# A 16-stage hybrid network on one core: order of the weight loads, loading of x, two attention openings, and a connection network in three bf16 parts

## What is computed

```
L0a mamba block + small MLP    L0f ternary layer     L0b attention, 16 narrow heads   L0g ternary layer
L1a linear attention           L1f connection net    L1b attention, 64-wide heads     L1g connection net
L2a one-head attention         L2f top-2 experts     L2b causal narrow attention      L2g top-2 experts
L3a mamba block                L3f gated (SiLU) net  L3b ReLU attention by sorting    L3g gated net
```

```python
def _conn_dense(kernel_bool, x):
    w = jnp.where(kernel_bool, jnp.float32(1.0), jnp.float32(-1.0))
    return x @ w
h = jnp.concatenate([x, -x], axis=-1)
h = s0 * _conn_dense(k0, h)          # 256 -> 512
h = jax.nn.relu(h) * 2
h = s1 * _conn_dense(k1, h)          # 512 -> 512
h = jax.nn.relu(h) * 2
h = s2 * _conn_dense(k2, h)          # 512 -> 128
```

## Time and profile before

| | us |
|---|---|
| runs: median (lowest, highest) of 3 | 3164.71 (3163.57, 3168.61) |
| the profiled execution's own time | 3165.05 |
| its span, first to last instruction | 3163.5 |
| mean granted clock of TensorE | 0.927 |

### The profile page before, as it was taken

One profiled execution on the slowest core, in us unless ns is written; L12 is line 12 of the kernel. 1 busy time (PEld: TensorE's weight loads), 2 busy tenths in 40 slices (PEclk: granted clock), 3 DMA queues, 4 the chain that ended last, 5 costly groups with the idle time before them and its releaser, 6 DMA issues. The chain is left out here.

```text
span 3163.5 us, 33520 instructions
## 1 busy us (share of the span) xinstructions
PE 2570.9 (81%) x11730; PEld 1095.1 (35%) x11738; DVE 1586.3 (50%) x2507; ACT 1446.3 (46%) x2392; POOL 677.6 (21%) x644
## 2 busy tenths in 40 slices
PE   3777788999789789768767787889997897897677
PEld 1231244544344234223222213445443442342232
DVE  3967543555121631695649585245442117217955
ACT  3544614555334354554545355155552444445454
POOL 1732010000001521371227311000000024115520
PEclk9898989999979899899889989999998898998998
DMA  3002000000010210000000010000000102100000
GB/s 122 1 1 73 8 1 1 1 1 1 1 53 1 76 59 0 0 1 1 1 15 1 25 56 1 1 1 1 1 1 0 53 1 81 54 0 1 0 1 7
DMA packets 36751, 55.68 MB, mean 18 GB/s; under 512 B 7648, under 2 KB 19936, under 8 KB 36576
## 3 DMA queue, kind: packets, MB, share of 16 engines
q1 hardware_dynamic: 32224, 49.53, 4.8%
q10 hardware_dynamic: 4352, 3.94, 0.4%
HBM read 39.54 MB, written 13.63 MB: 17 GB/s over the span
## 5 line engine op out<-in xcount | busy, mean ns | idle before, releaser
L522 POOL TENSOR_TENSOR xs<-xs,L2f_part 128x512 f32<-128x512 f32 x32 | 40.5, 1264 | 1181.8 <-DVE L2f_part L511 1181.8
L1942 ACT ACTIVATE L1b_pr<-ps,L1b_mneg 128x512 f32<-128x512 f32 x256 | 173.7, 684 | 197.0 <-DVE L1b_mneg L1981 197.0
L1979 DVE TENSOR_REDUCE L1b_m<-ps 128x2 f32<-128x1024 f32 x128 | 156.8, 1225 | 114.9 <-PE ps L1846 111.2
L1649 ACT ACTIVATE L0b_pt<-ps 128x1024 f32<-128x1024 f32 x128 | 129.3, 1024 | 117.9 <-PE ps L1549 115.8
L90 ACT ACT_TABLE_LOAD x44 | 56.5, 1283 | 268.0 <-PEq L224 41.4
L1737 DVE TENSOR_REDUCE L0b_mx<-ps 128x1 f32<-128x512 f32 x256 | 159.0, 684 | 37.0 <-PE ps L1536 35.5
L1226 POOL TENSOR_TENSOR L3a_db<-L3a_du,L3a_bs 128x1024 f32<-128x1024 f32 x64 | 150.4, 2360 | 114.0 <-DVE L3a_du L1337 68.1
L1226 POOL TENSOR_TENSOR L0a_db<-L0a_du,L0a_bs 128x1024 f32<-128x1024 f32 x64 | 150.5, 2359 | 112.5 <-DVE L0a_du L1337 66.0
L2005 DVE COPY L1b_prt<-ps 128x512 f32<-128x512 f32 x128 | 88.5, 692 | 124.9 <-PE ps L1857 124.6
L1354 DVE TENSOR_TENSOR_SCAN L0a_hs<-ps,L0a_db 128x1024 f32<-128x1024 f32 x64 | 146.1, 2283 | 5.4 <-ACT ps L1149 5.4
L1354 DVE TENSOR_TENSOR_SCAN L3a_hs<-ps,L3a_db 128x1024 f32<-128x1024 f32 x64 | 146.1, 2282 | 5.0 <-ACT ps L1149 5.0
(11 more groups left out here) (566 smaller groups left out, 5274.2 us busy)
## 6 DMA issues: line engine op xcount, KB each, us to landing
L2f_w<-expert_dram SPq DMA_DIRECT2D x32, 256.0 KB, 3.0
L2g_w<-expert_dram SPq DMA_DIRECT2D x32, 256.0 KB, 3.0
weights<-w_dram SPq DMA_DIRECT2D x7, 987.5 KB, 10.7
L0b_qs<-stack_dram SPq DMA_DIRECT2D x32, 96.0 KB, 2.2
stack_dram<-L0b_cut SPq DMA_DIRECT2D x24, 128.0 KB, 2.1
L2b_qs<-stack_dram SPq DMA_DIRECT2D x32, 96.0 KB, 2.2
stack_dram<-L2b_cut SPq DMA_DIRECT2D x24, 128.0 KB, 2.2
L0b_ks<-stack_dram SPq DMA_DIRECT2D x28, 96.0 KB, 2.2
```

What stands on the lines that cost most here:

```text
L1649: act.activation(pt[:, n % 3, 2 * half:2 * half + 2, q0:T], g.ps[:, 2 * (s % 2):2 * (s % 2) + 2, q0:T], ACT.Exp).then_inc(prob, 1)
L1942: act.activation(pr[:, s % 2, h, :], g.ps[:, 2 * (s % 2) + h, :], ACT.Exp, bias=mneg[:, s % 2, h:h + 1], accum_out=total[:, u % 2, t, h:h ...
L1979: dve.tensor_reduce(m[:, s % 2, :], g.ps[:, 2 * (s % 2):2 * (s % 2) + 2, :], AX.X, ALU.max).then_inc(max_raw, 1)
```

## The change

**Start.** The packed weights are sorted: those that `prepare` needs (1013 columns), those of L0a and the normalisation (3551), the rest (11229). SP loads the first, then x, then the second, then the rest in six pieces (`REST`); `prepare` waits for the first two pieces of weights and for x, and `ternary_ffn` makes SP wait for the rest (`g.rest_loaded`). The connections are loaded in L1a and converted by POOL at that stage's end, the integers in L1b, again by POOL, in each pass. The taps and output weights of a mamba stage are scaled by POOL at its start, into `taps` (the space of `dt[:, 1]`) and `out_w`. SP's order before, then in the change (`ISA` are cleared semaphores):

The diff, cut to its core (`...` where lines are left out; the rest of the L3b part renames banks and semaphores):

```diff
 def prepare(g, x_dram, wd, cut):
...
+                sp.dma_start(g.weights[:, 0:cut[0]], wd[:, 0:cut[0]]).then_inc(loaded, 16)
+                sp.dma_start(g.xs[:, :, :], x_dram[0:NB, :, :].rearrange("b p t -> p b t")).then_inc(x_loaded, 16)
+                sp.dma_start(g.weights[:, cut[0]:cut[1]], wd[:, cut[0]:cut[1]]).then_inc(loaded, 16)
+                for c in range(REST):
+                    a, z = (cut[1] + (n - cut[1]) * k // REST for k in (c, c + 1))
+                    sp.dma_start(g.weights[:, a:z], wd[:, a:z]).then_inc(g.rest_loaded, 16)
+                sp.wait_ge(x_loaded, 16)
...
-                dve.wait_ge(loaded, 16 * cut)
+                dve.wait_ge(loaded, 32)
...
 def connection_ffn(g, name):
...
+        def split_x(eng, b, part, left):
+            for p in range(PARTS):
+                if p >= 1:
+                    eng.wait_ge(part, p)
+                    eng.tensor_tensor(ln.sq[:, b, :], g.xn[:, b, :] if p == 1 else ln.sq[:, b, :], xc[:, b, p - 1, :], ALU.subtract).then_inc(left, 1)
+                    eng.wait_ge(left, p)
+                eng.tensor_copy(xc[:, b, p, :], ln.sq[:, b, :] if p else g.xn[:, b, :]).then_inc(part, 1)
...
+                pe.wait_ge(whole_in, FT)
+                pe.wait_ge(hi, FT)
+                for k in range(FT):
+                    for p in range(PARTS):
+                        wait_part(k, p)
+                        for f in range(FT):
+                            mm = pe.matmul(g.ps[:, f, :], w1[:, k * FF + f * P:k * FF + (f + 1) * P], h[:, 0, 0, k, p, :],
+                                           start=(k == 0 and p == 0), stop=(k == FT - 1 and p == PARTS - 1))
...
+                for n in range(2 * TILES):
+                    layer, b, f = tile(n)
+                    act.wait_ge(hidden, n + 1)
+                    act.activation(h[:, layer, b, f, 0, :], g.ps[:, 4 * b + f, :], ACT.Relu, scale=g.s2x[:, layer:layer + 1]).then_inc(hi, 1)
+                    if n >= DEEP:
+                        act.wait_ge(rest_in, n - DEEP + 1)
+                    act.activation(whole[:, n % DEEP, :], g.ps[:, 4 * b + f, :], ACT.Relu, scale=g.s2x[:, layer:layer + 1]).then_inc(whole_in, 1)
...
+                def leave(n):
+                    layer, b, f = tile(n)
+                    dve.wait_ge(whole_in, n + 1)
+                    if n >= DEEP:
+                        dve.wait_ge(lo, n - DEEP + 1)
+                    dve.tensor_tensor(rest[:, n % DEEP, :], whole[:, n % DEEP, :], h[:, layer, b, f, 0, :], ALU.subtract).then_inc(rest_in, 1)
...
 def gated_ffn(g, name, x_dram=None, out_dram=None, i=None):
...
+                if last:
+                    for b in range(NB):
+                        sp.wait_ge(added, b + 1)
+                        sp.dma_start(out_dram[bass.ds(i * NB + b, 1), :, :].rearrange("b p t -> (b p) t"), g.xn[:, b, :]).then_inc(stored, 16)
+                        sp.dma_start(g.xs[:, b, :], x_dram[bass.ds(NB + b - i * NB, 1), :, :].rearrange("b p t -> (b p) t")).then_inc(x_loaded, 16)
+                    sp.wait_ge(stored, 16 * NB)
+                    sp.wait_ge(x_loaded, 16 * NB)
...
 def mamba(g, name, w, variant):
...
+                rows = g.w(w + "_taps").rearrange("p (j e) -> p j e", j=4)
+                pool.tensor_tensor(taps[:, :, :], rows, bcast(g.w(w + "_in", 0, 2 * P), 1, 4), ALU.mult).then_inc(folded, 1)
+                pool.tensor_scalar(out_w[:, :], g.w(w + "_out"), 0.5, None, ALU.mult).then_inc(folded, 1)
...
 def narrow_attention(g, name, w, causal, scale):
...
-                    if s >= LAG and (s - LAG) % 2 == 0:
-                        products((s - LAG) // 2)
                     for a in range(tops_before(s), tops_before(s + 1)):
                         top_scores(e, a)
                         e += 1
+                    if s >= LAG and (s - LAG) % 2 == 0:
+                        products((s - LAG) // 2)
...
 def wide_attention(g, name):
...
+        OPENING = (SMALL, PV, 4, 5, SMALL, PV)
...
+                    bank = SMALL
+                    if b == NB - 1:
+                        bank = LAST
+                        pe.wait_ge(turned_dve, STEPS)
+                        pe.wait_ge(at_ready, UN - 1)
...
 def relu_attention(g, name):
...
+                take_q(0)
+                take_turned(3)
+                gelu(2)
+                gelu(3)
+                take_z(2)
+                take_z(3)
+                load_exp_ln(g.nc)
...
-                    if n == 11:
+                    if n == 15:
+                        spread(4)
                         turn_keys(1)
...
+                    if u == 1:
+                        scale_q(1)
```

More of the change, by code:

```diff
@@ L22 @@
 EXP_LN_SET = 6
+REST = 6
 ALU = mybir.AluOpType
@@ L292, in _ @@
+                pe.wait_ge(whole_in, TILES)
+                for p in range(PARTS):
+                    wait_part(TILES - 1, p)
+                for f in range(FT):
+                    for k in range(FT):
+                        for p in range(PARTS):
+                            mm = pe.matmul(g.ps[:, 4 + f, :], w1[:, k * FF + f * P:k * FF + (f + 1) * P], h[:, 0, 1, k, p, :],
+                                           start=(k == 0 and p == 0), stop=(k == FT - 1 and p == PARTS - 1))
                     mm.then_inc(hidden, 1)
@@ L308, in _ @@
                 ln.scalar(act)
-                for layer in range(2):
-                    for b in range(NB):
-                        act.wait_ge(hidden, layer * NB + b + 1)
-                        act.activation(h[:, b, :, :], g.ps[:, 4 * b:4 * b + FT, :], ACT.Relu, scale=g.s2x[:, layer:layer + 1]).then_inc(relu, 1)
+                for n in range(2 * TILES):
[5 more added lines that the diff above has]
+                    act.activation(whole[:, n % DEEP, :], g.ps[:, 4 * b + f, :], ACT.Relu, scale=g.s2x[:, layer:layer + 1]).then_inc(whole_in, 1)
+            @block.gpsimd
+            def _(pool):
+                pool.wait_ge(ln.done, NB)
+                split_x(pool, 1, y_part, y_rest)
+                for n in range(2 * TILES):
+                    layer, b, f = tile(n)
+                    pool.wait_ge(rest_in, n + 1)
+                    pool.tensor_copy(h[:, layer, b, f, 1, :], rest[:, n % DEEP, :]).then_inc(mid, 1)
             @block.vector
@@ L2611, in _pack @@
     put("r3_b2", b2.reshape(128, 1))
+    first = ("f0_w", "f0_alpha", "f0_b", "f1_s", "bf_consts", "mean_mat", "m0_alog", "m3_alog")
+    early = first + ("centre", "ident", "eps5", "eps6")
+    rank = lambda name: 0 if name in first else 1 if name in early or name.startswith("m0_") else 2
+    parts.sort(key=lambda part: rank(part[0]))
+    cut = [sum(m.shape[1] for name, m in parts if rank(name) <= k) for k in range(2)]
     cols, at = {}, 0
```

354 lines of the change are left out of this document (194 added, 160 removed).

## The result

The changed kernel takes **3074.07 us** (median of 4 runs, 3070.64 to 3075.35) against 3164.86 (3163.57 to 3168.61): a ratio of 0.971, with a 95% interval from 0.9693 to 0.9726. That is 90.8 less, where 75.5 were forecast, and it lies in the range. The profiled execution has a span of 3069.1, the shortest of the four (the others 3071.6 to 3073.8), so the two spans differ by 94.4.

The account below looks back on a forecast made before the run. No engine was taken to bound the whole kernel, so each part was priced in its own stage: 25.4 + 4.4 + 16 + 24 + 2.4 + 4 - 0.7 = 75.5 less, a span of 3088.0 and a time of 3089 us, range 3070 to 3108.

Parts of the forecast that it names:

- The start: Before the loop: weights loaded in order of need let PE start at 14.5, 25.4 us less (22.9 to 26.4).
- the meeting of the passes: Between the passes: x loaded behind the last sum, 9.8 in place of 14.2, 4.4 us less (3.4 to 5.5).
- rival C: At the start: queued loads share the DMA engines evenly, so early pieces don't come early; 3101 us, chance 0.05.
- L1b: Wide attention: opening of 7.8 instead of 18.6, 24 us less in two passes; idle at its end gone, 2.4 less.
- Rival D: In L1b: it opens with half clock because the normalisation before it leaves PE idle; 3101 us, chance 0.09.
- The network: Connection network: 48 fp32 products become 144 in bf16, 4.0 us less per stage, 16 less in four.
- Rival A: In the network: the tiles' chain through ACT, DVE and POOL becomes the bound; 3105 us, chance 0.13.
- Rival B: In the network: TensorE stays at the lower clock through the bf16 products, slower than before; 3203 us, chance 0.03.
- L0b: Narrow stage: column-maximum products ahead of probability products, same number over two slots; 0, with 8 us either way.
- L2b: Narrow stage with the same reordering as L0b; 0, with 8 us either way.
- L1a and L2a: Two stages forecast at 0; the connections' casts, moved to POOL behind L1a, were priced at 0.
- L3b: ReLU stage's opening: DVE's wait of 5.57 becomes about three of 3, 4 us less in two passes (10 less to 6 more).

Follow-up runs that it names:

- the kernel with the split order: The changed kernel with column-maximum products again behind the probability products in L2b alone, the new order kept in L0b: 3065.27 us, ratio 0.9684.
- Both improvements: The changed kernel with another opening of the connection network and three of ACT's steps in L3b moved: 3053.85 us, ratio 0.9666 to the kernel before.

## Why the prediction was right, and where it was not

**The start (-25.4, it was -27.0) and the meeting of the passes (-4.4, it was -5.2)** were right in mechanism and order; the ternary part, the way to PE and the clearing were each a few tenths shorter. The early pieces land early, at 10.01, while the rest is queued behind them; that excludes rival C. With the second half of what I cited from the Trainium skill (DMA: Bandwidth & Descriptors, "Queues, rings and completion order"), the order within a ring, the trace agrees. The taps, priced at 0, cost nothing (L0a 179.8 / 180.3 before, 179.6 / 180.5 after).

**L1b (-24 and -2.4, it was -27.2 together)** was right step by step, 7.8 for 7.8. Rival D did not come about: the clock stayed at its upper level, 1.00 in the opening. The forecast had the reason only half, since I spoke of six projections in one bank; in the run with the old opening the clock also lies at 0.50 through the stretch with these waits, and each product takes 2.08 instead of 1.13.

**The network (-16, it was -14.3; undone +14.2)** came out near, with one step of a wrong kind. In L1f 36.2 lie between the first product of layer 0 and the last sum, within the 35 to 39 that I had named. I said that layer 1 and the output would take 35.0 - 8.9 = 26.1 from layer 1's first product to the last sum; it is 423.19 to 449.33, 26.1. I put the opening at 8.9 and added 2.5 for half clock; it is 11.7 from the normalised sequence. But the clock was the smaller part: the first cast waits behind the second normalisation, and DVE's operations take up to three times as long beside POOL's. Without POOL, and with the first cast moved up, the opening takes 8.6 and needs no allowance at all. The Trainium skill (SBUF — State Buffer, "Who interferes with whom") says that DVE and GpSimd share one pair of ports under an exclusive lock: a DVE instruction in a two-port mode, or one with two SBUF inputs beside a GpSimd instruction that reads SBUF, waits when GpSimd's was issued first. The cast of 1.26 that ends 0.28 behind POOL's subtraction agrees with it. Of the 3.1 between 11.7 and 8.6 the first cast's wait is 1.2. The two subtractions and two casts behind it took 2.2 longer beside POOL, and the second normalisation, which now stands between them, takes 0.6 of that back; 0.3 is left for the half clock. I had added 0.7 for this over the whole program. One bound does not follow from its terms: with products 0.255 apart and half clock at once, the stage comes to 8.9 + 30.6 + 0.3 + 2.5 = 42.3, or 3 more in four stages and not 6 less.

Rival A did not come: no product of layer 1 waits for a part. Rival B did not either. The window of layers 1 and 2 reads

```profile
423.20:448.50 25.30, 25.30 (x118) 11.34 (x119) 20.71 (x30) 14.33 (x24) 12.87 (x14) 1.00 0.00 1
```

and against the other rule that I cited from the Trainium skill (TensorE: Matmul & The Clock Gate, "A second HAM failure mode: psum-queue depth-cycling"), bf16 products of 512 columns that go through four banks show no swing of the clock here.

**L0b (0, it was -18.8)** is the step that failed, and it is as large as the whole difference between 75.5 and the 94.4 of the two spans. I wrote that over two slots the same products stand in the same number, and that DVE's idle time comes from PE's total. The number does not matter; what matters is what stands right ahead of the one product that must wait for another engine's last result. DVE's 37.0 of idle ahead of its maxima was a hint, since it was PE that ended it; what decides is the row of the transposition, for which I had not asked. PE alone is idle for 19.3 ahead of it before and for 6.6 after. **L2b (0, it was +6.9)**: its transposition lost that cover. PE's busy time in the stage is the same in the two profiles (178.5 and 178.6 in two passes), and its idle rose from 59.3 to 66.0, which is nearly all of the 6.9. Over all profiles PE's idle is 29.4 to 31.1 per pass in the six passes with the old order and 31.7 to 33.8 in the 18 with the new one and the lead of 33, means of 30.2 and 32.6. The two ranges don't meet, so an idle of 2.4 per pass is the order's. The length of the stage is not as clear, because PE's busy time varies from 87.8 to 93.5 with the clock: it took from 118.7 to 122.0 with the old order (mean 120.3) and from 121.0 to 125.5 with the new one (mean 122.8). The time of the kernel with the split order, some 8 under the changed kernel's two medians, speaks for a gain of this size, but I call what the order is worth in time likely and not shown. Both improvements with the split order weren't run together.

**L1a and L2a (0, they were -5.0 and -3.6)**: the instructions on PE are the same, and so nearly is its idle (L1a 15.8 and 15.5 per pass, L2a 28.8 and 28.7). What fell is PE's busy time, with a higher granted clock: in pass 1 of L1a from 47.1 at 0.87 to 42.8 at 0.96. The connections' casts on POOL, priced at 0, cost nothing in L1a. I had no term for the clock here. L1a took 60.2 or less in the first pass of 11 of the 13 profiles with the new start, but in the second pass of only 5, so the gain is neither this one execution's alone nor reliable, and of the kernel before there is one profile. What sets the clock there stays open, and that it helped the sum is luck.

**L3b (-4, it was +0.8)**: the 4.8 of the earlier first ReLU were right. I put the three waits at 3 each in place of one of 5.57, 3.4 more; they were 5.3, 3.3 and 4.2, and with the smaller waits of both kernels DVE's idle between its first and last ReLU rose by 4.3. ReLU operations beside POOL are no part of it, since both kernels have them.

Without L0b the spans differ by 75.6, and 75.5 were forecast. That agreement is in part luck: L2b, L3b and the network fell short by 6.9 + 4.8 + 1.7 = 13.4, and the start, L1b, the meeting, L1a, L2a and the rest brought 13.5 more than forecast.

## What to carry to other kernels

An engine that works in order pays for a wait where the waiting instruction stands: look for the instruction that needs another engine's last result, and put independent work right ahead of it. Counting products per slot does not find it, its idle row does; take that row for one engine at a time, or a weight load and its product are counted twice. When work is spread over idle engines, price DVE's operations beside POOL's, not alone. And cut a trace into stages on both sides of a change before explaining the total, and each stage into PE's busy time and idle: here the clock moved the first and the order of instructions mainly the second. Take two or three executions of the same kernel for what a stage does by itself.

## What the runs showed of the hardware

**DVE beside POOL.** A cast of 128x512 from fp32 to bf16 in SBUF took 0.42 alone and 1.26 beside POOL's subtraction; a subtraction 0.69 and 0.98; twelve ReLU operations 4.84 and 8.06. It shows as a longer duration and not as idle time, so that no list of waits names it.

**The clock takes different ways through the same thin stretch.** In the profiles of all these kernels L1a took 58.3 to 62.9 and L2a 61.0 to 63.0, with the same instructions on PE, and L2b 118.6 to 125.5. In L1a PE's idle stayed between 15.1 and 15.8, while its busy time went from 42.8 at a clock of 0.96 to 47.1 at 0.87. The length also differed between the two passes of one execution. On a kernel like this, differences of up to 4.5 in one stage of a single profile say nothing without the clock beside them.
